# TensorE's order in a slot: two transposes ahead of projections, the output product behind the last token product

## What is computed

```python
patches = x[:, idx, :]                                  # 93 patches of 16 rows, step 8
h = einsum('bnpd,edp->bne', patches, Wr) + b            # tokens, 64 x 93 x 128
# attention on layernorm(layernorm(h)): causal, ALiBi bias, 8 heads of 64
q, k, v = (conv3(w1 @ xn, wd) for w1, wd in ...)        # 1x1 product, then 3 taps along the tokens
h = h + softmax(q k^T / 8 + bias) v @ wout.T
# mixture of 16 experts, top 2, on layernorm(h)
h_e = mean over the tokens of expert e of silu(w1_e x); y_e = w2_e h_e
h = h + sum over the 2 chosen experts of routing_w * y_e
```

## Time and profile before

| | |
|---|---|
| time, median of 3 runs | 767.68 us (765.91 to 769.25) |
| the profiled execution | 768.05 us, its span 766.4 us |
| TensorE busy | 702.5 us (92%) |
| ScalarE busy | 608.4 us (79%) |
| VectorE busy | 564.7 us (74%) |
| GpSimd busy | 376.4 us (49%) |
| mean granted TensorE clock | 0.966 |
| chain that ended last | PE 47%, DVE 23%, ACT 18%, issue 6%, DMA 3% |

### The profile page before, as it was taken

How to read it: one execution, slowest core, us unless ns; L and a number is a source line. 1 busy time by engine, 2 the same in 40 slices (tenths; PEclk the granted TensorE clock), 3 DMA queues, 4 the chain that set the end, 5 groups by cost and what they waited for, 6 DMA issues and landing times.

```text
span 766.4 us, 21100 instructions
## 1 busy us (share of the span) xinstructions
PE 702.5 (92%) x6514; PEld 628.8 (82%) x6514; DVE 564.7 (74%) x1579; ACT 608.4 (79%) x2022; POOL 376.4 (49%) x390
## 2 busy tenths in 40 slices
PE   4689999999999999999999999988787878999986
PEld 4678888888898898889888898867675777999983
DVE  2166777888788877878788878888865468888865
ACT  3457898989898999889898998878776576899950
POOL 3553335666557566666656666544344354122200
PEclk9889999999999999999999999999999579999996
DMA  5522124241212112222212122020224012222205
GB/s 173 164 63 80 42 96 138 70 129 52 72 52 54 50 53 61 57 59 53 68 50 56 49 54 74 10 73 14 64 51 174 18 46 75 57 64 64 65 14 160
DMA packets 44273, 53.99 MB, mean 70 GB/s; under 512 B 13651, under 2 KB 31251, under 8 KB 43696
## 3 DMA queue, kind: packets, MB, share of 16 engines
q1 hardware_dynamic: 30048, 38.84, 17.7%
q0 software_dynamic: 12544, 12.87, 6.2%
q10 hardware_dynamic: 1616, 1.48, 0.6%
HBM read 42.69 MB, written 10.26 MB: 69 GB/s over the span
## 4 chain that ended last, share of the span: by engine, by line
PE 47%; DVE 23%; ACT 18%; issue 6%; DMA 3%; POOL 1%; DVEq 0%; ACTq 0%; SPq 0%
ACT prob L805 11%; PE psTP L450 5%; DVE qkv L979 5%; PE psTP L451 5%; PE psTP L452 5%; PE psSO L707 4%; DVE qkv L982 4%; PE psTP L707 4%; DVE prob L1095 4%; PE psSO L541 4%; PE psSO L652 3%; PE psSO L574 3%; PE psTP L522 3%; ACT qkv L785 3%; DMA x_raw<-in_x 3%
## 5 line engine op out<-in xcount | busy, mean ns | idle before, releaser
L1328 POOL DMA_INDIRECT expert_rows<-hn,slot x128 | 167.9, 1311 | 64.9 <-DVE slot L1175 33.1
L805 ACT ACTIVATE prob<-psSO,rmin 93x93 f32<-93x93 f32 x512 | 151.9, 355 | 6.9 <-DVE rmin L1065 6.8
L1261 POOL TENSOR_TENSOR x_lo<-x_raw,x_hi 128x752 fp32r<-128x752 f32 x64 | 115.1, 1799 | 54.6 <-ACT x_hi L777 54.2
L979 DVE SCALAR_TENSOR_TENSOR qkv<-psTP,taps,qkv 128x368 f32<-128x368 f32 x192 | 112.5, 586 | 20.7 <-ACT qkv L785 20.6
L785 ACT ACTIVATE qkv<-psTP,taps 128x372 f32<-128x372 f32 x192 | 113.2, 589 | 10.6 <-PE psTP L452 10.0
L982 DVE SCALAR_TENSOR_TENSOR qkv<-psTP,taps,qkv 128x364 f32<-128x364 f32 x192 | 114.6, 597 | 6.8
L450 PE MATMUL psTP<-x_hi,wtok_hi 128*128 128x376 f32 x256 | 98.7, 385 | 11.3 <-DVE wtok_lo L967 9.2
L805 ACT ACTIVATION_READ_ACCUMULATOR prob<-psSO,rmin 93x1 f32 x512 | 98.8, 193 | 0.0
L452 PE MATMUL psTP<-x_hi,wtok_lo 128*128 128x376 f32 x256 | 87.6, 342 | 0.0
L451 PE MATMUL psTP<-x_lo,wtok_hi 128*128 128x376 f32 x256 | 87.5, 342 | 0.0
L1090 DVE RECIPROCAL psSO<-psSO 93x8 f32<-93x8 f32 x64 | 13.6, 212 | 96.1 <-ACT prob L805 96.1
(11 more groups left out here) (194 smaller groups left out, 1679.1 us busy)
## 6 DMA issues: line engine op xcount, KB each, us to landing
x_raw<-in_x SPq DMA_DIRECT2D x64, 376.0 KB
w1s<-in_w POOLq DMA_DIRECT2D x8, 512.0 KB
w<-in_w SPq DMA_DIRECT2D x4, 1024.0 KB
out<-resid SPq DMA_DIRECT2D x16, 160.0 KB, 2.7
xsE<-expert_rows SPq DMA_DIRECT2D x36, 64.0 KB, 2.1
xs<-expert_rows SPq DMA_DIRECT2D x36, 64.0 KB, 1.8
xs<-expert_rows POOLq DMA_DIRECT2D x36, 64.0 KB, 2.1
expert_rows<-hn,slot POOLq DMA_INDIRECT x128
```

The lines of the kernel that those rows point to most:

```text
L805: i = nc.scalar.activation(prob[:, a, hh, :], psS[:NT, a, hh * NT:(hh + 1) * NT], ACT.Exp, bias=rmin[:, a, hh:hh + 1], scale=-1.0, accum_o ...
L979: nc.vector.scalar_tensor_tensor(dst[:, :, 1:NT], src[:, :, 0:NT - 1], taps[:, k, 1:2], dst[:, :, 1:NT], ALU.mult, ALU.add).then_inc(tap1_ ...
L1261: nc.gpsimd.tensor_tensor(x_lo[u][:, 0:PIECE], x_raw[u][:, :], x_hi[u][:, 0:PIECE].bitcast(F32), ALU.subtract)\
L1328: nc.gpsimd.indirect_dma_start(rows, bass.IndirectOffsetOnAxis(slot[1 - u][:, c:c + 1], 0), hn[1 - u][:, c % GB, :], None)\
```

## The change

Three moves in TensorE's sequence of a slot, and none on another engine. The transposes of `hn` (slot 2) come ahead of `proj(3s)` instead of behind it. The transposes of the values come ahead of `proj(3s+1)`, right behind `weigh`. Token product 3 comes ahead of the output product, which so is the last large piece of a slot.

```diff
@@ step of TensorE
-                    if f.proj:
-                        proj(t, u, f, 3 * s)
                     if f.gate and s == 2:
                         wait(pe, hn_ready, t - 3)
                         wait(pe, base_done, t - 4)
...
                         mm.then_inc(hnT_tr, 1)
+                    if f.proj:
+                        proj(t, u, f, 3 * s)
...
                     if q is not None and s == 0:
                         turn_quad(q)
+                    if f.attn:
+                        turn_values(t, u, f, s, n)
                     if f.proj:
                         proj(t, u, f, 3 * s + 1)
-                    if f.attn:
-                        turn_values(t, u, f, s, n)
                     if f.tok:
                         tok_taps(t, s, 1, 1)
...
                     if f.proj:
                         proj(t, u, f, 3 * s + 2)
+                    if f.tok:
+                        tok_taps(t, s, 3, 1)
                     if prev:
                         pe.wait_ge(a_evac, n)
...
                         mm.then_inc(out_mm, 1)
                     if q is not None and s == 0:
                         up_quad(q, 0, QUAD)
-                    if f.tok:
-                        tok_taps(t, s, 3, 1)
```

## The result

The changed kernel takes 782.04 us (median of 4 runs, 780.03 to 783.89) against 768.09 us of before in the same comparison: ratio 1.0185, interval 1.0158 to 1.0213. It is slower by 14 us. The profiled execution took 782.07 us, its span 780.4, so it stands 14.02 above the one of before.

What follows compares the result with a forecast made beforehand. Busy TensorE, and a circle through ScalarE's tap2(3s+1) and VectorE back to TensorE with hardly any slack, were taken as bounds. 12 x 0.97 = 11.6 plus 0.4 gives +12.0 us on 768.05: 780 us, range 771 to 786.

Steps and rivals of the forecast that it cites:

- Changes of type: TensorE's switches between fp32 and fp32r: runs of fp32r products fall from four to two a slot, claimed gain 0.
- rival A: TensorE alone sets the pace and opening an fp32r run costs 104 ns: 10 us less, 758 us; chance 0.07.
- The way out of `weigh`: Instruction behind `weigh`, now L564 instead of L450: 0 taken, bounds a gain of 0.19 and a loss of 0.08 us a slot.
- The walk: TensorE's lateness through one step's four slots: +0.27, +0.57, +0.57, then +0.97 us at the next L601.
- Which wait: TensorE's `turn_prob` of the next slot waits for VectorE's add, with slack of 0.22, 0.19 and 0.76 us.
- `hn` at 0: Moved `hn` transposes in slot 2 delay `proj(6)` and its `tap2` by 0.32 us, hidden by later `proj(7)`: cost 0.
- The signs: Expected if right: L601s about 35.3 us apart, new ScalarE idle time near 0.4 us, longer VectorE idle, TensorE waits at L536 or L555.
- three waits of 0.08: Upper bound: each new wait also costs TensorE's restart, 0.08 us longer for four transposes, three a step; 12 x 1.25 = +15 us.
- the circle's own range: Times by the bounds if the circle of TensorE, ScalarE and VectorE holds as walked: 773.5 to 785 us; chance 0.78.
- The 0.4 for the rest: Loss added for step 15, the first slots and the steps from 16 without token products: 0.4 us.
- rival C: TensorE's granted clock also falls in the full steps, 10.7 us of lost clock on top: 790 or more; chance 0.03.

Runs made afterwards that it cites:

- the last pair of kernels: Kernel before with tap2(3s+1) behind the exponentials, routing behind rmin, values first; second also puts token product 3 ahead of output product: 750.53 and 750.32 us.

## Why the prediction was right

- *The forecast*: 780, measured 782.0, in the range. The direction holds, and so does the mechanism: a late `tap2(3s+1)` that comes back to TensorE through VectorE. That the total came so near is in part luck, since two terms were off in opposite directions. Steps 3 to 14 lost 10.7 us and not 11.6, and all the rest 3.3 us and not 0.4.
- *Changes of type cost nothing*: right. Product last alone and in the last pair of kernels gave nothing, and rival A's gain of 10 us, 5 us for one run fewer in a slot, is excluded by them.
- *The way out of `weigh`*: I took 0 between -0.19 and +0.08; it is -0.03 a slot.
- *The walk*: from L601 to slot 1's L555 it took 7.99 us instead of 7.75, +0.24 (I said 0.27); on to slot 2's 8.22 instead of 7.93, +0.29 (0.30); to slot 3's 8.79 instead of 8.89, -0.10 (0); to the next L601 10.21 instead of 9.80, +0.41 (0.40). Together 0.84 against 0.97. The step that was off is slot 2: it got a little shorter, 8.83 us instead of 8.88 between its scores and those of slot 3; the rest of the 0.10 is the 0.04 us by which its own L555 started later behind the scores.
- *Which wait*: this part of the mechanism was wrong. I let the add decide at L555. TensorE waits earlier, for the product at L536, and at L555 only for the last bit: from L541 to L555 it takes 0.87 us (322.95 to 323.82) instead of 0.83. The product stands ahead of the add on VectorE and is late by as much, so the size came out nearly the same. I had not priced L536, where the slack before was 0.3 us (the product ended at 306.98 and 314.94, the scores started at 307.30 and 315.23), and where two products behind a wait add 0.49 us in the chain instead of 0.32.
- *`hn` at 0*: right inside this change, since the values' delay is larger in slot 2; but alone it costs 0.28 us a step, so it was hidden work and not free. My sentence named the cover and didn't say what it costs when the cover is gone, which is why the run without values surprised me.
- *The signs*: ScalarE's new idle time was to be near 0.4 us in slots 0 to 2; it is 0.24, 0.32 and none, as in slot 2 `hnT` is late with the rest. VectorE's idle time before the reciprocal grew by 0.35, 0.26 and 0.20 us in these slots. L450 behind L564 adds 0.17, as said.
- *A sum that was off*: three waits of 0.08 on top of 0.97 are 1.21 a step and not 1.25, so that bound is +14.5, and the circle's own range ends at 783 and not 785. The forecast and the range given do not hang on it.
- *The 0.4 for the rest*: too small, as said; nearly all of the 3.3 us was lost from step 15 on. Of these 2.65 is the clock of rival C, in another place than I put it: not in the full steps, where it stayed 1.00, but in step 18. I gave C 0.03 and priced it at 10 us on top; a small piece of it happened beside the forecast, and no run shows that the change is its cause.

## What to carry to other kernels

When two engines are nearly full, look for the circle that runs through both and back, and measure its slack at the places where one is released by the other within 0.05 us. An edit that delays such a handover by more than the slack costs the difference in every turn, even though each engine does the same work. The same reading shows the cheaper edit: on the engine in the middle, let what the circle waits for go first, and what nobody waits for behind it.

## What the hardware showed that I had not expected

- The first fp32r product behind the fp32 output product or the fp32 transposes of the values adds 0.17 to 0.18 us in the chain, as much as one inside a run: that change costs nothing here.
- Leaving the 64-wide products of `weigh` costs 0.19 us into an fp32r product (0.36 against 0.17) and 0.16 into the four fp32 transposes (0.60 against 0.44).
- The granted clock fell to 0.50 (1.2 GHz) two slots earlier in step 18 in the profiled execution of the change than in that of before, with the same work of TensorE in the slot ahead, and cost 2.65 us. The cause is open.
